# Moving six shared-expert tiles behind the expert blocks, and taking norm-weight multiplies off GpSimd

## What is computed

```python
x = x + tanh(g_xattn[0]) * cross_attention(ctx_2048, layernorm(x), mask)
x = x + tanh(g_ffn[0])   * moe(layernorm(x))      # 64 experts, top 8, inner width 176, and 2 shared experts
x = x + tanh(g_xattn[1]) * attention(layernorm(x), ctx_2048)   # 16 heads of 16, keys: 77 of the context + 256
x = x + tanh(g_ffn[1])   * ffn(x_of_this_layer)   # F = 1024, norm_w, 8 LoRA experts of rank 16, top 2
# in moe:  rw = routed weights (T, 64);  out = sum_e rw[:, e] * mlp(x, Wg[e], Wu[e], Wd[e]) + mlp(x, Sg, Su, Sd)
# in ffn:  nx = x * rsqrt(mean(x * x) + eps) * norm_w;  nx goes into w1, w3, the gate and the LoRA factors a1, a3
```

## Time and profile before

| what | value |
|---|---|
| median of 3 runs | 1524.48 us (1524.08 to 1525.07) |
| the profiled execution, its own time | 1539.73 us |
| its span | 1538.0 us |
| PE busy | 1365.9 us, 89% of the span |
| PE weight loads busy | 1074.9 us, 70% |
| DVE busy | 870.8 us, 57% |
| ACT busy | 704.9 us, 46% |
| POOL busy | 560.3 us, 36% |

### The profile page before, as it was taken

The page is one execution under the profiler, slowest core; times in us unless marked ns, Lnnn a source line. Parts: engine busy times, 40 slices in busy tenths (PEclk is TensorE's granted clock), DMA queues, the critical chain, the costliest instruction groups (busy, mean ns, idle before and its releaser), DMA issues. The chain is left out here.

```text
span 1538.0 us, 31436 instructions
## 1 busy us (share of the span) xinstructions
PE 1365.9 (89%) x8188; PEld 1074.9 (70%) x8189; DVE 870.8 (57%) x2394; ACT 704.9 (46%) x1879; POOL 560.3 (36%) x622
## 2 busy tenths in 40 slices
PE   4988997999999999999166998898997899999998
PEld 3876665777777777777044666676775699999997
DVE  7969971333333333333446676666668576666666
ACT  2533232444444444444044776666775544444443
POOL 1002554333333333331657666866434111111110
PEclk8968998999999999999568999999998999999999
DMA  4034103777565656643432112221021000000000
GB/s 103 0 90 134 32 11 104 217 211 231 173 209 177 186 161 203 211 116 91 130 104 79 46 45 60 66 69 51 9 64 48 8 15 15 15 14 14 14 7 15
DMA packets 98384, 136.40 MB, mean 89 GB/s; under 512 B 19899, under 2 KB 82307, under 8 KB 98275
## 3 DMA queue, kind: packets, MB, share of 16 engines
q1 hardware_dynamic: 55315, 61.41, 13.4%
q0 software_dynamic: 15456, 48.62, 11.8%
q10 hardware_dynamic: 27504, 25.05, 4.8%
HBM read 103.01 MB, written 32.01 MB: 88 GB/s over the span
## 5 line engine op out<-in xcount | busy, mean ns | idle before, releaser
L1240 PE MATMUL ps<-wgu,xT 128*128 (+1 forms) x892 | 308.0, 469 | 2.3 <-ACT xT L1023 1.0
L762 POOL DMA_INDIRECT xg<-n_rows,idx x191 | 180.6, 945 | 296.7 <-DVE wS L2054 208.5
L1240 PE MATMUL ps<-wdn,hT 88*128 (+1 forms) x892 | 227.8, 380 | 3.8 <-DVE hT L2060 2.9
L2189 DVE TENSOR_REDUCE nmx<-ps 128x1 f32<-128x333 f32 x256 | 127.2, 498 | 132.0 <-PE ps L1240 120.1
L1240 PEld LDWEIGHTS ps<-wgu,xT 128*128 128x128 f32 x892 | 154.8, 193 | 53.9 <-issue 5.1
L1118 ACT ACTIVATE pD<-ps,nmx 128x333 f32<-128x333 f32 x256 | 138.8, 545 | 99.9 <-DVE nmx L2189 79.5
L2057 DVE TENSOR_TENSOR hC<-sg,ps 128x176 f32<-128x176 f32 x191 | 64.5, 338 | 179.3 <-ACT sg L1074 168.8
L1240 PEld LDWEIGHTS ps<-wdn,hT 88*128 88x128 f32 x892 | 153.0, 190 | 18.1 <-issue 3.8
L1532 PE MATMUL ps<-ident,pD 128*128 128x128 f32 x768 | 131.3, 282 | 36.3 <-DVE pT L2195 28.4
L2060 DVE COPY hT<-ps 88x256 f32<-88x256 f32 x191 | 80.4, 421 | 136.5 <-issue 86.4
L779 POOL DMA_INDIRECT yg<-y_rows,slotG x128 | 123.5, 965 | 80.6 <-issue 29.6
(11 more groups left out here) (302 smaller groups left out, 3063.7 us busy)
## 6 DMA issues: line engine op xcount, KB each, us to landing
y_rows<-yC ACTq DMA_DIRECT2D x191, 128.0 KB
wgu<-in_wgu SPq DMA_DIRECT2D x64, 352.0 KB
wdn<-in_wdn SPq DMA_DIRECT2D x64, 176.0 KB
xg<-n_rows,idx POOLq DMA_INDIRECT x191
kraw<-in_kD SPq DMA_DIRECT2D x8, 308.0 KB
x<-in_x SPq DMA_DIRECT2D x4, 512.0 KB, 4.5
n_rows<-nB SPq DMA_DIRECT2D x4, 512.0 KB, 3.4
xg<-n_rows SPq DMA_DIRECT2D x16, 128.0 KB, 2.1
```

The costliest lines, as they stand in the source:

```text
L762: pool.indirect_dma_start(out=xg[:, b % XS, :], out_offset=None, in_=n1_rows, in_offset=bass.IndirectOffsetOnAxis(ap=idx[:, b:b + 1], axis ...
L1240: return pe.matmul(o, lhsT, rhs, start=start, stop=stop, **kw)
L2189: dve.tensor_reduce(nmx[:, k:k + 1], ps[:, score_bank(k), 0:NK1], AX, ALU.max, negate=True).then_inc(d_mx, 1)
```

## The change

1. Only 10 shared tiles (`NSE`) run before the experts. The other six (`NSL`) run behind the last expert block, in 12 half steps, one shared expert each (`late_up` and `late_down` on PE, `late_silu` and `late_xT` on ACT, `c_hidden` and `late_add` on DVE). The shared weights have tensors of their own, which live until then; SP loads the six tiles' rows into `xg`. The last store of a block's output stands on ACT behind the first two late silus and the second late copy.
2. The multiply by the norm weight is gone from `split` and `scale_gates` is gone; `e_copy` on DVE, a copy from PSUM, becomes a product with the norm weight (16 instructions in all).
3. Subtract of the split and first add of `sum_rows` are each in two halves. Matrices 2 to 5 are split in batch 5, one behind each group's reciprocal, and 6 to 11 in batch 6, two behind each of the first three; SP's `load_raw` moves with them.
4. `select` is in 11 parts behind steps 1 to 14, and the steps behind it are 2 to 6 later.
5. `yg` lies elsewhere in memory, which the split matrices 6 to 9 overlay.

```diff
+NSE = 10
+NSL = NT - NSE
...
-        SELECT_AT = (1, 3, 4, 5, 6)
-        HEAD_HIGH_AT, HEAD_HALF_AT, HEAD_TURN_AT, HEAD_RANKS_AT, HEAD_LOW_AT, HEAD_COPY_AT = 4, 13, 16, 19, 21, 23
+        SELECT_AT = (1, 3, 4, 5, 6, 7, 9, 10, 12, 13, 14)
+        HEAD_HIGH_AT, HEAD_HALF_AT, HEAD_TURN_AT, HEAD_RANKS_AT, HEAD_LOW_AT, HEAD_COPY_AT = 4, 19, 21, 23, 25, 27
...
             for b in range(BATCH):
                 if b + 2 < BATCH:
                     load_ctx(b + 2, b % 2)
-                if b in (2, 3):
-                    load_raw(b + 2)
+                if b == BATCH - 3:
+                    load_raw(4)
+                    load_raw(5)
                 if b == BATCH - 2:
                     sp.wait_ge(k_red, 2 * NT)
-                    for k in range(6, 10):
+                    for k in range(6, 12):
                         load_raw(k)
-                if b == BATCH - 1:
-                    load_raw(10)
-                    load_raw(11)
...
+            for t in range(2):
+                onehots(t, t)
+            for t in range(FILL_AT, NSE):
+                s_step(t, t % 2, t // 2)
                 for s in range(2):
-                    onehots(2 * t - 2 * FILL_AT + 2 + s, 2 - 2 * r + s)
...
+                    n = 2 * (t - FILL_AT) + 2 + s
+                    onehots(n, n % OHS)
+            for t in range(2 * (NSE - FILL_AT) + 2, NT):
+                onehots(t, t % OHS)
+                if t == 2 * (NSE - FILL_AT) + 2:
+                    s_sum(NSE - 1, (NSE - 1) % 2)
...
-                if k < 6:
-                    own.link(pool.tensor_scalar(raw, raw, nwP[:, (k - 2) % DC:(k - 2) % DC + 1], None, ALU.mult))
...
-                pool.tensor_tensor(low, raw, high.bitcast(F32), ALU.subtract).then_inc(r_done, 1)
...
+                own.step(pool.tensor_tensor(part(low, 0), part(raw, 0), part(high, 0).bitcast(F32), ALU.subtract))
+                pool.tensor_tensor(part(low, 1), part(raw, 1), part(high, 1).bitcast(F32), ALU.subtract).then_inc(r_done, 1)
...
-                    if b == BATCH - 2:
-                        split(6 + g)
+                    if b == BATCH - 3:
+                        split(2 + g)
+                    if b == BATCH - 2 and g < NG1 - 1:
+                        split(6 + 2 * g)
+                        split(7 + 2 * g)
...
-                if 1 <= b <= 4:
-                    split(b + 1)
...
-                    split(10)
-                    split(11)
...
+            late_xT(0)
+            for m in range(2 * NSL):
+                late_silu(m)
+                if m % 2 and m // 2 + 1 < NSL:
+                    late_xT(m // 2 + 1)
+                if m < 2:
+                    c_step(NRUN + m, NBLK // BLOCKS - 1, NRUN + m - NBLK + BLOCKS)
...
-                dve.tensor_copy(nTs[:, :, r * P:(r + 1) * P], ps[:, bank, at:at + D].rearrange("p (c n) -> p c n", c=DC)).then_inc(e_in, 1)
+                dve.wait_ge(ld_e, 16 * 5)
+                dve.tensor_tensor(nTs[:, :, r * P:(r + 1) * P], ps[:, bank, at:at + D].rearrange("p (c n) -> p c n", c=DC),
+                                  nwP[:].unsqueeze(2).broadcast_to([P, DC, P]), ALU.mult).then_inc(e_in, 1)
...
+            FIRST_LATE = ((6, 7), (), (8, 9), (10, 11))
+            for r in range(TB):
+                for part in range(2):
+                    d_reduce(0, 0, r, part)
+                    if part:
+                        d_sum(0, 0, r)
+                    late_hidden(*FIRST_LATE[2 * r + part])
+            late_add(NSL - 1)
+            d_ve(0, 0)
```

260 lines of the change are left out of this document (153 added, 107 removed).

## The result

The changed kernel takes 1522.8 us (median of 12 runs, 1516.4 to 1528.6) against 1525.6 us before (12 runs, 1522.9 to 1532.0). The ratio is 0.9975, with a 95% interval of 0.9963 to 0.9987: faster by 3.8 us (the two medians alone lie 2.8 apart), where 13.4 had been forecast, and above the range of 1501 to 1522. (A difference of 3 us is about what the measurement can tell.)

A forecast was written before the change was run, and what follows sets the result against it. PE was taken to bound experts and last layer, leaving time ahead of the experts, in the gap and in some batches; -16.5 + 11.5 - 11.5 + 8.6 + 1 - 6.5 = -13.4 from 1524.5 gave 1511 us, range 1501 to 1522.

The forecast's parts named there:

- Ahead of the experts: Start of tables to first expert gather: fewer shared tiles beside the tables and before the gather, -16.5 us.
- In the gap: Between experts and first scores: twelve late half steps delay last store, variance and scores, +11.5 us.
- the slow end of +13.2: In the gap: six late half steps lose 0.7 us each on a slow clock, +13.2 instead of +9.0 us.
- Batches 2 to 4: Attention batches 2 to 4: without splits on POOL they shorten to about batch 1's length, -11.5 us.
- Batches 5 and 6: End of batch 5 +8.6 us for a new wait; splits in batch 6 +1 us.
- The wait for matrix 4: End of batch 5: load behind batch 7's context load delays POOL's split and last `recX`; PE idles 6.4 to 6.6 us.
- the splits in pairs: Batch 6: two splits at a time ahead of a power and later `recX`, +1 us, between 0 and +4.
- Batch 7: Last attention batch: splits gone and `select` spread over 14 steps remove PE's excess idle, -6.5 us.
- A: Rival: late tiles nearly free; gap costs 7 us, batch 5 costs 5, time 1503 us; chance 0.17.
- B: Rival: POOL never set batches 2 to 4, so that gain and half of batch 7's are lost, 1525.7 us; chance 0.07.
- C: Rival: in batches 5 and 6 split(5) and the pairs also hold up reciprocals, another 9 us, 1520 us; chance 0.09.
- D: Rival: gap half steps run singly at 1.2 GHz, +35 us, 1534.5 us; sign: scores over 28 us late; chance 0.07.

The follow-up runs named there:

- b_again: The kernel before, unchanged, measured and profiled a second time: 1526.5 us, ratio 1.0001; profiled execution 1526.1 us.
- best2: Changed kernel, matrix 4/5 loads first, splits 8/9 behind power, POOL's gap order changed, half steps 6/7 before DVE's first sum: 0.9987 with stalls; 0.9861, 0.9843 without.
- pool_only: The kernel before with only parts 2 to 4 of the change, all 16 shared tiles ahead of the experts: 1520.3 us, ratio 0.9975.
- late_only: The changed kernel without parts 2 to 4, so only the late tiles (parts 1 and 5): 1528.6 us, ratio 1.0011.
- raw_first: The changed kernel with SP's loads of matrices 4 and 5 ahead of the context load of batch 7: 1515.1 us, ratio 0.9930.
- raw_pow: The changed kernel with loads of matrices 4 and 5 first and, in batch 6, splits 8 and 9 behind the power: 1510.5 us, ratio 0.9905.
- a_again: The changed kernel, unchanged, measured again in two runs: 1514 and 1519 us, ratio 0.9934.
- the job with stalls: Runs on one chip with long idle times without a releaser in all four profiles: kernel before 1541.4 us, changed kernel, unchanged, 1549.5 us (1.0061).

## Why the prediction was right and wrong

**Ahead of the experts: right.** -15.4 for -16.5, by the tables that have no shared tile beside them and the shared tiles that no longer stand ahead of the gather: 16 tables from 162.68 to 213.76 instead of 163.68 to 217.06, and from the list of rows to the gather 2.2 us instead of 14.2. (In the working, 8 x 0.5 is 4.0 and not 4.2.)

**In the gap: the step that failed.** +15.7 for +11.5. Two parts of it were wrong. The sentence "Before, PE then waited for DVE's keys until 783.72, 3.2 us later than `place`; now `place` is the later one" took a stall of ACT for the kernel's ordinary course. That credit of 3.2 us does not exist: the end of `place` follows the variance by the same 16 to 17 us in both kernels, and every microsecond by which the variance is late reaches the scores (from the variance to the scores 23.5 us in b_again, 23.6 after). And the variance was taken to follow from the second tile's rows, which DVE comes to only 2.5 us after they were forecast to land, busy with half steps behind the first sum; with a longer chain behind them that makes 3.6 us. best2 bears it out: with half steps 6 and 7 ahead of the first sum the variance came 34.2 us behind the first gather instead of 39.6. The forecast of +9.0 on a fast clock, with these 3.2 and 3.6 us, gives the measured 15.7 within 0.1.

What the forecast held for the clock covered 2.5 of it by luck (the middle of 9.0 and 13.2 is 11.1; 11.5 was taken). By the rule of the Trainium skill that the prediction named ("TensorE: Matmul & The Clock Gate", section "Loop structure matters more than you think") the slow end of +13.2 would have held. It is nearer to what was measured than the middle, but not by the clock: of the late products behind the second tile's rows only one up and one down product ran slow (2.03 us at 746.61 and 1.87 at 748.86, where the others take 1.35 and 1.03), 1.5 us and not 4.2. The last store was right (+3.1 forecast, the experts' stretch 2.5 longer), batch 0 gave 1.4 back. The listed terms of the chain add to 14.0, not 13.55; that is inside the 775.4 to 776 that was used.

**Batches 2 to 4: right.** -13.5 for -11.5: 47.4, 48.5, 47.4 us, and no residual add above 0.48 us in batch 2. pool_only shows the same three lengths and late_only the old ones (51.7, 53.1, 51.7), so it is POOL's relief and not the late tiles. How much of it is the splits moved away and how much the halved adds was not separated.

**Batches 5 and 6: the waits are there, the size was wrong.** +13.8 for +9.6, as large a miss as the gap's. The wait for matrix 4 came as forecast: PE idle for 5.5 us, where 6.4 to 6.6 had been forecast, and the clock at about 0.57 for 6 us behind it. raw_first takes it away, and 4.4 us stay, where the splits in pairs had been put at +1 (up to +4). That term is the one that was mis-sized: the second pair keeps the power back, DVE waits 2.7 us for it and PE 3.2, and in three profiles of four the clock falls behind it. Even at the full clock, in raw_pow, with the pair behind the power, batch 6 takes 2.2 us more than before. The short batch 6 of a_again (46.6, against 46.4 before) is no sign that the pairs are free, since PE had done 38 of its instructions before the cut.

**Batch 7: right**, -5.5 for -6.5: the idle of 7.53 us, which b_again has too, is gone. Here too the spread `select` and the splits moved away were not separated.

**Not in the sum:** the clock. Batch 1 (+1.7) and the last layer (+2.2) have PE's instructions of before. In the profiles without stalls batch 1 takes about 48.5 or about 50.2 us, at a clock of 1.00 or 0.97, and the last layer 320.7 to 322.9, whatever the kernel. The changed kernel's own three such profiles have the longer batch 1 twice; that its new idle times bring this about is argued, not shown. The prediction had named a last layer over 2 us off as a sign that a part of its sum is missing, and this is that part.

**The rivals.** A and B did not happen: the gap cost more than 7 us, and batches 2 to 4 got shorter. C's time, 1520, is the nearest to the measured one, in part by luck: the pairs cost more than forecast, as C has it, but by keeping back the power and not a reciprocal, and half of the miss is in the gap. D (half steps one after another at the low clock) did not happen: the scores are 15.7 us late against the start of the experts, under its mark of 28, and most late products ran at the full clock. In the job with stalls the sign that D forecast came about by another mechanism. The range was too narrow because its bounds were taken term by term from one execution, and that execution was 1% above the median; the text noted it and took a difference to carry over. It does not where the disturbance sits in the very stretch that is costed.

## What to carry to other kernels

When the profiled execution is slower than the median, look for idle times without a releaser ("remote", "issue"), and compare them with a second profile, before using a stretch as the base of a sum: a slack behind such a time is not there in ordinary runs. Work moved into a gap is not free because an engine idles there: it delays what closes the gap on the other engines. Here reordering POOL's and SP's queues around each deadline brought 18 to 20 us more (0.9975 to 0.985) and moving the tiles nothing that the times show, and an order that is right for one time of the variance is wrong for another. A split or cast on GpSimd should stand neither ahead of a power that DVE waits for nor beside DVE's short steps behind it.
